# A recurrence's capping and its own-term product move from VectorE to GpSimd, in a one-core AdaLN, attention and FFN kernel

## The reference, cut to what matters

```python
def bi_wkv(r, k, v, w, u, time_emb):          # called with k = v = fside
    ek  = exp(min(k, 30.0))
    ekv = ek * v
    # forward and reverse scans over the 512 positions:
    #   a = a * decay + ekv_t ;  b = b * decay + ek_t
    euk = exp(min(u + k, 30.0))
    num = nf + nb - ekv + euk * v
    den = df + db - ek + euk
    return sigmoid(r) * num / max(den, 1e-8) * gain

x = x + attention(bi_wkv(x, fside, fside, w1, u1, cond), w_qkv, w_o)
x = x + ffn(bi_wkv(x, fside, fside, w2, u2, cond), w_gate, w_up, w_down)
```

## Time and profile before

| | |
|---|---|
| median of 3 runs | 939.11 us (938.11 to 940.47) |
| the profiled execution, its own time | 939.99 us |
| its span, first to last instruction | 938.3 us |
| mean granted TensorE clock | 0.922 of full speed |
| time outside the span | 1.7 us |

### The profile page before, as it was taken

One profiled execution on the slowest core, in us unless ns is written; L12 is line 12 of the kernel. 1 busy time (PEld: TensorE's weight loads), 2 busy tenths in 40 slices (PEclk: granted clock), 3 DMA queues, 4 the chain that ended last, 5 costly groups with the idle time before them and its releaser, 6 DMA issues.

```text
span 938.3 us, 10306 instructions
## 1 busy us (share of the span) xinstructions
PE 752.8 (80%) x3752; PEld 372.9 (40%) x3793; DVE 767.3 (82%) x1057; ACT 468.7 (50%) x694; POOL 73.5 (8%) x149
## 2 busy tenths in 40 slices
PE   2646617698879899897898998877989999995756
PEld 1212203245544344454443444544434446552322
DVE  2999998989997779889978798799877995525466
ACT  5755644448665262476653624766536234441330
POOL 1000000111100002111000021110000211100000
PEclk9777757999999999999999999999999999998778
DMA  8622210445400003654000036540000373300001
GB/s 316 250 67 95 101 56 12 101 102 159 100 12 23 1 12 90 191 146 113 12 23 1 12 89 191 147 113 12 23 1 12 80 190 90 90 1 0 1 0 45
DMA packets 30306, 72.25 MB, mean 77 GB/s; under 512 B 5808, under 2 KB 5808, under 8 KB 28464
## 3 DMA queue, kind: packets, MB, share of 16 engines
q1 hardware_dynamic: 19792, 46.94, 17.0%
q0 software_dynamic: 6144, 16.79, 7.6%
q10 hardware_dynamic: 4320, 7.87, 2.5%
HBM read 33.82 MB, written 4.19 MB: 41 GB/s over the span
## 4 chain that ended last, share of the span: by engine, by line
PE 42%; DVE 31%; issue 9%; ACT 7%; DMA 6%; SPq 4%; POOL 1%; DVEq 0%; ACTq 0%
PE bank L1308 12%; DMA stacks<-rows 5%; PE bank L1320 5%; PE bank L1247 4%; PE bank L1161 4%; PE bank L1236 4%; PE bank L1218 3%; SPq L300 3%; DVE negmax L963 3%; PE bank L1187 2%; ACT region L504 2%; PE bank L1220 2%; DVE fn L847 2%; PE bank L1153 1%; DVE num L861 1%
## 5 line engine op out<-in xcount | busy, mean ns | idle before, releaser
L963 DVE TENSOR_REDUCE negmax<-bank 128x4 f32<-128x512 f32 (+2 forms) x96 | 98.7, 1036 | 40.9 <-PE bank L1194 22.6
L504 ACT ACTIVATE region<-bank 128x384 f32<-128x384 f32 (+1 forms) x192 | 95.5, 523 | 66.1 <-PE bank L1221 63.5
L1218 PE MATMUL bank<-stacks 128*128 128x512 f32 (+3 forms) x256 | 104.8, 416 | 29.2 <-ACT region L504 22.1
L300 POOL DMA_DIRECT2D stacks<-rows x128 | 69.5, 551 | 735.3 <-DVE region L746 351.5
L1161 PE MATMUL bank<-h,wqkv 128*128 128x512 f32 x256 | 115.7, 603 | 7.6 <-DVE region L1114 4.2
L1187 PE MATMUL bank<-stacks 128*128 128x128 f32 (+3 forms) x256 | 81.0, 411 | 10.2 <-DMA stacks<-rows 5.8
L1308 PE MATMUL bank<-region,gate_q 128*128 128x512 bf16 x244 | 62.9, 397 | 23.4 <-DVE region L746 23.0
L1161 PEld LDWEIGHTS bank<-h,wqkv 128*128 128x128 f32 x256 | 48.7, 194 | 66.1 <-issue 55.7
L1218 PEld LDWEIGHTS bank<-stacks 128*128 128x128 f32 x256 | 51.0, 199 | 58.9 <-ACT region L504 39.2
L1114 DVE TENSOR_TENSOR region<-bank,region 128x1024 f32<-128x1024 f32 x32 | 39.1, 1222 | 42.9 <-PE bank L1308 42.9
L1220 PE MATMUL bank<-maxrow,pick 128*128 128x384 bf16 (+3 forms) x236 | 74.0, 314 | 0.0
(11 more groups left out here) (158 smaller groups left out, 1380.4 us busy)
## 6 DMA issues: line engine op xcount, KB each, us to landing
stacks<-rows SPq DMA_DIRECT2D x128, 128.0 KB, 4.0
stacks<-rows POOLq DMA_DIRECT2D x128, 128.0 KB, 4.6
kt<-in_fside ACTq DMA_DIRECT2D x30, 256.0 KB, 3.2
h<-in_x SPq DMA_DIRECT2D x4, 1024.0 KB, 5.7
region<-in_w_gate SPq DMA_DIRECT2D x4, 1024.0 KB, 11.7
xt<-in_x SPq DMA_DIRECT2D x4, 1024.0 KB, 7.5
region<-in_w_up SPq DMA_DIRECT2D x4, 1024.0 KB, 5.7
region<-in_w_down SPq DMA_DIRECT2D x4, 1024.0 KB, 4.7
```

What stands on the lines that cost most here:

```text
L300: eng.dma_start(stacks[HD * r:HD * r + HD, at:at + 2, i, :].bitcast(F32), rows[mine, q:k + 1:k - q, :]).then_inc(stacked[s][i], 16)
L504: nc.scalar.activation(probs[:, i, P_AT[tiles[0]]:P_AT[tiles[0]] + columns], bank[4 + n % 2][:, 0:columns], ACT.Exp, scale=SCALE).then_inc ...
L963: nc.vector.tensor_reduce(o, scored, AX_X, ALU.max, negate=True).then_inc(max_taken, 1)
L1218: nc.tensor.matmul(o, ks[s][:, i, P * t:P * t + P], qs[s][:, i, P * t:T], start=True, stop=False, skip_group_check=True)
```

## The change

On POOL two functions are new. `cap` moves there from DVE as it was. `own_product` caps `eu` in place and writes the product with k over the tile of k; it needs `ekv_ready`, since DVE's `ekv = ek * k` must have read k first. On DVE `add_own` keeps two plain additions. ACT's `load_k` may overwrite k only after `num` has been summed, and moves behind `reciprocals`, at every place where the two stand together. `own_exp` waits also for the product of the unit before. DVE's `ekv = ek * k` no longer waits for `num_ready`.

```diff
+            def cap(b, u):
+                if not live(b, u):
+                    return
+                U = unit(b, u)[2]
+                pool.wait_ge(k_in[u % 2], k_loaded(b, u))
+                if U:
+                    pool.wait_ge(fwd_ready, 2 * U)
+                nc.gpsimd.tensor_scalar(ek[:, :], kt[:, u % 2, :], EXP_CAP, None, ALU.min).then_inc(capped, 1)
+
+            def own_product(b, u):
+                if not live(b, u):
+                    return
+                U = unit(b, u)[2]
+                pool.wait_ge(eu_ready, U + 1)
+                nc.gpsimd.tensor_scalar(eu[:, :], eu[:, :], CAPPED_EXP, None, ALU.min).then_inc(eu_capped, 1)
+                pool.wait_ge(ekv_ready, U + 1)
+                pool.wait_ge(eu_capped, U + 1)
+                nc.gpsimd.tensor_tensor(kt[:, u % 2, :], eu[:, :], kt[:, u % 2, :], ALU.mult).then_inc(euv_ready, 1)
+
+            cap(-1, CJ)
+            for u in range(CJ, 2 * CJ + 1):
+                own_product(-1, u)
+                cap(-1, u + 1)
+            own_product(-1, 9)
+            cap(-1, 10)
             pool.wait_ge(setup, SETUP_STEPS)
             pool.wait_ge(quartered, 2 * WC + 2)
             stack(pool, 0, 0, 2, HG)
+            own_product(-1, 10)
+            cap(-1, 11)
             for b in range(B):
                 pool.wait_ge(down_ready, 1 + b)
                 stack(pool, b, 1, 2, HG)
+                own_product(b, 3)
+                cap(b, 4)
                 stack(pool, b, 2, 2, HG)
+                own_product(b, 4)
+                cap(b, 5)
+                own_product(b, 5)
+                cap(b, 6)
                 stack(pool, b, 3, 2, HG)
+                for u in range(6, 11):
+                    own_product(b, u)
+                    cap(b, u + 1)
                 if b + 1 < B:
                     pool.wait_ge(iq_ready, b * FC + 2)
                     stack(pool, b + 1, 0, 2, HG)
...
                 if U:
                     act.wait_ge(summed, U)
+                    act.wait_ge(euv_ready, U)
                 nc.scalar.activation(eu[:, :], kt[:, u % 2, :], ACT.Exp,
...
-                    act.wait_ge(summed, unit(b, u)[2] + 1)
+                    act.wait_ge(num_ready, unit(b, u)[2] + 1)
                     act.dma_start(kt[:, u % 2, :], fside_tile(b, u + 2)).then_inc(k_in[u % 2], 16)
...
+                reciprocals(b, 4)
                 load_k(b, 4)
-                reciprocals(b, 4)
                 own_exp(b, 5)
...
                     if U:
-                        dve.wait_ge(num_ready, U)
+                        dve.wait_ge(fwd_ready, 2 * U)
                     nc.vector.tensor_tensor(ekv[:, :], ek[:, :], kt[:, u % 2, :], ALU.mult).then_inc(ekv_ready, 1)
...
-                dve.wait_ge(eu_ready, U + 1)
-                nc.vector.scalar_tensor_tensor(ekv[:, :], eu[:, :], CAPPED_EXP, kt[:, u % 2, :], ALU.min, ALU.mult).then_inc(euv_ready, 1)
+                dve.wait_ge(eu_capped, U + 1)
                 dve.wait_ge(bwd_ready, 2 * U + 1)
-                nc.vector.scalar_tensor_tensor(den[:, :], eu[:, :], CAPPED_EXP, den[:, :], ALU.min, ALU.add).then_inc(summed, 1)
+                nc.vector.tensor_tensor(den[:, :], eu[:, :], den[:, :], ALU.add).then_inc(summed, 1)
                 dve.wait_ge(euv_ready, U + 1)
                 dve.wait_ge(bwd_ready, 2 * U + 2)
-                nc.vector.tensor_tensor(num[:, :], num[:, :], ekv[:, :], ALU.add).then_inc(num_ready, 1)
+                nc.vector.tensor_tensor(num[:, :], num[:, :], kt[:, u % 2, :], ALU.add).then_inc(num_ready, 1)
```

More of the change, by code:

```diff
@@ L187, in adaln_attention_ffn @@
         eu_ready = sem("eu_ready")
+        eu_capped = sem("eu_capped")
         fwd_ready = sem("fwd_ready")
@@ L525, in turn @@
                 low_parts(b, 1)
+                reciprocals(b, 2)
                 load_k(b, 2)
-                reciprocals(b, 2)
                 own_exp(b, 3)
@@ L538, in turn @@
                 exps(b, 0, 5, 8)
+                reciprocals(b, 3)
                 load_k(b, 3)
-                reciprocals(b, 3)
                 own_exp(b, 4)
@@ L564, in turn @@
                 copy_maxima(b, 2)
+                reciprocals(b, 5)
                 load_k(b, 5)
-                reciprocals(b, 5)
                 own_exp(b, 6)
@@ L575, in turn @@
                 exps(b, 2, 9, 12)
+                reciprocals(b, 6)
                 load_k(b, 6)
-                reciprocals(b, 6)
                 own_exp(b, 7)
@@ L587, in turn @@
                 exps(b, 3, 6, 12)
+                reciprocals(b, 7)
                 load_k(b, 7)
-                reciprocals(b, 7)
                 own_exp(b, 8)
@@ L594, in turn @@
                 cap_exp(b, 9)
+                reciprocals(b, 8)
                 load_k(b, 8)
-                reciprocals(b, 8)
                 own_exp(b, 9)
@@ L676, in _ @@
                 else:
+                    reciprocals(-1, u)
                     load_k(-1, u)
-                    reciprocals(-1, u)
                     own_exp(-1, u + 1)
@@ L689, in _ @@
                 if n % 2 == 0:
+                    reciprocals(-1, n // 2 + 4)
                     load_k(-1, n // 2 + 4)
-                    reciprocals(-1, n // 2 + 4)
                     own_exp(-1, n // 2 + 5)
@@ L821, in decay @@
                 return decay_all[:, batch_of(b, u), CJ * second + j:CJ * second + j + 1]
[L823 to L829, removed]
-                    dve.wait_ge(fwd_ready, 2 * U)
-                nc.vector.tensor_scalar(ek[:, :], kt[:, u % 2, :], EXP_CAP, None, ALU.min).then_inc(capped, 1)
             def forward(b, u, f):
@@ L898, in _ @@
             ch = Chain(dve, wq_steps, 0, 0)
-            cap(-1, CJ)
             top_magnitude(ch, 0, True)
@@ L913, in _ @@
                         finish(-1, u - 1)
-                    cap(-1, u + 1)
                 else:
@@ L925, in _ @@
                     forward(-1, 8, c)
-                elif c == 2:
-                    cap(-1, 9)
             backward(-1, 8, 0)
@@ L942, in _ @@
                         finish(-1, 8)
-                    cap(-1, 10 + k // 2)
                 round_weights(ch, first + k, first, rounded(first + c))
@@ L1012, in turn @@
                 late_lows(b)
-                cap(b, 4)
                 maxima(b, 1, 0)
@@ L1026, in turn @@
                 finish(b, 3)
-                cap(b, 5)
                 backward(b, 4, 0)
@@ L1039, in turn @@
                 maxima(b, 2, 3)
-                cap(b, 6)
                 backward(b, 5, 0)
@@ L1053, in turn @@
                 finish(b, 5)
-                cap(b, 7)
                 backward(b, 6, 0)
@@ L1066, in turn @@
                 finish(b, 6)
-                cap(b, 8)
                 backward(b, 7, 0)
@@ L1074, in turn @@
                 finish(b, 7)
-                cap(b, 9)
                 normalise(b, 3)
@@ L1099, in turn @@
                         forward(b, 9, 1)
-                        cap(b, 10)
                     else:
@@ L1123, in turn @@
                         forward(b, 10, f - 3)
-                    elif f == 5:
-                        cap(b, 11)
                 raise_top(b, FJ // 2 - 1)
```

## The result

The changed kernel takes **962.53 us** (median of 4 runs, 959.86 to 964.5) against 939.79 us for the kernel before in the same session (4 runs): a ratio of 1.0242, 95% interval 1.0212 to 1.0272. It is slower by 2.4%. 961 had been forecast.

What follows compares the result with a forecast made beforehand. VectorE (82% busy) and PE (80%) share the chain; VectorE counts in the weight stage and attention. Weight stage 4.1 plus three turns of 6.0 gave 22.1 on 939.99, 962.1; the median 0.9 lower, 961 us; range 926 to 980.

Steps and rivals of the forecast that it cites:

- rivals A: Whole kernel: no exclusion beyond the two-port forms, GpSimd's work hidden everywhere; 12.5 us faster, 927 us; chance 0.24.
- C's every-microsecond price: Whole kernel, upper end of the main case: VectorE pays every GpSimd microsecond, 2.52 us a unit; +47, 986 us.
- B's picture: Whole kernel: exclusion, but VectorE keeps the turn and GpSimd waits; 4.7 us faster, 934 us; chance 0.13.
- The rule of exclusion: GpSimd instructions reading SBUF and VectorE instructions with two SBUF inputs run one after the other; full VectorE pays GpSimd's length.
- 0.63 us for a tensor_scalar: Each one-tile GpSimd instruction of 128x512, estimated from mask rows at 0.87 ns a column; 2.33 us a unit with the product.
- my upper end: GpSimd's time per unit at most 2.52 us, taking the product as twice a one-tile instruction.
- Weight stage +4.1: Weight stage: six units, 14.0 us of GpSimd, charged 9.3 less the gain of 5.2 us.
- Turn, 413 to 459, +1.9: Attention stretch of each turn: 8.7 us of GpSimd, half charged as 4.35, less the gain of 2.45 us.
- 459 to 485, +0.5: Units 7 and 8 in each turn: PE's stretch, VectorE has slack until the last normalisation; 0.5 us lost.
- Attention's end +1.6: Each turn: unit 9's capping and product delay the second scan and unit 10's cap, so ACT waits 1.6 us.
- Rounding +2.0: Each turn's rounding: 2.33 us of GpSimd fall on back-to-back VectorE work; fourth piece has slack 0.1; 2.0 us lost.
- Waits and order at no cost: Later load of k, the added wait and copies behind caps cost nothing; closest, the copies after unit 6's cap, about 1 us late.

Runs made afterwards that it cites:

- the idle products and tensor_scalars: Kernel before plus GpSimd instructions nobody reads in the weight stage: 946.79 us with both kinds, 943.55 with products only, 947.04 with tensor_scalars only.
- the middle units alone: Changed kernel with the weight stage's units and each turn's two end units back on VectorE: 935.21 us, ratio 0.9969; repeated, 936.93 us.
- nothing moved: Changed kernel with all caps and own products back on VectorE, leaving only the new order on ScalarE: 944.39 us, ratio 1.0071 to the kernel before.

## Why the prediction was right, and which terms were not

The time (961 against 962.5), the sign and the mechanism held; rivals A and B fell, C's every-microsecond price too, though B's picture, VectorE going on and GpSimd kept waiting, is what most tensor_scalars show. But that the sum came so near is luck: several terms were wrong and cancelled, and 5.1 us of clock stood in none. By its steps:

- **The rule of exclusion, both tiles in SBUF.** Held: the idle products and tensor_scalars stretch VectorE with no dependence between them, and the maxima from PSUM did not change. The Trainium skill (SBUF — State Buffer, Who interferes with whom) has whichever of the two comes first hold the shared ports for its whole instruction; the trace agrees nearly for the product (the scan behind it is stretched by 1.0 of its 1.28 us) and not for the tensor_scalar, 1.48 us long, of which VectorE pays 0.3 to 0.5.
- **0.63 us for a tensor_scalar.** Mis-sized: the mask's slope does not carry over. Unhindered it takes 1.48 to 1.49 us, and 1.97 to 2.04 on average. The product, 1.07 in the forecast, takes 1.27; the 1.07 has a slip in it, for half a column's time more than 0.63 is 0.85, and only a whole one's gives 1.07. The unit is 4.2 us unhindered, not 2.33, above my upper end. The two errors, too short and too fully charged, met in a similar charge: 2 x 0.48 + 0.77 = 1.7 us a unit by the idle instructions.
- **Weight stage +4.1.** It was +7.0 at its end. The first unit's cap at the program's start and the last unit's instructions were left out of the six units that I counted; seven products and eight caps run there.
- **Turn, 413 to 459, +1.9, and 459 to 485, +0.5.** It was nothing: from the turn's first row to the last split of the maxima 82.7 us before and 82.6 after in turn 1, and 250.4 and 249.5 over the three turns. VectorE is still nearly full there (lengths and columns as in the earlier trace rows):

```profile
433.00:473.00 40.00, 30.73 (x236) 17.23 (x234) 38.52 (x47) 24.34 (x46) 16.26 (x15) 0.96 0.29 74
```

So the charge and the gain came out level there, where 4.35 against 2.45 had been forecast. The kernels with the middle units alone show the same for all turns: moving these is no loss.
- **Attention's end +1.6.** It was 2.44. The chain has the links that were written, but the second scan was not pushed back by 1.7: it came 0.4 us later, kept its 1.19, and the product waited for it (2.24 us). The cap stood behind the product and started about where it had been forecast, by luck; it takes 1.49 us, not 0.63, and that is the missing 0.84, nearly.
- **Rounding +2.0.** It was 1.7, by 1.06 for the product and 0.29 for each tensor_scalar.
- **Missing: the granted clock.** F took 5.1 us over three turns, which no term held. TensorE's mean clock over the 35 us that hold the gate and up products was 1.00 in 16, 0.95 in 14 and 0.90 in none of the 30 turns of the ten kernels whose idle time before them was 2.3 to 3.4 us. In the four kernels with 3.5 to 4.7 us it was 1.00 in none, 0.95 in 5 and 0.90 in 7 of 12. In the changed kernel it was 0.90 in all three. So a longer wait at attention's end seems to be paid twice. The two go together, but no run varied the wait alone: the four kernels are also the ones with the end units' products on GpSimd. Within the first group the same idle time goes with either value; what decides there stays open.
- **Waits and order at no cost.** Not so for the order on ScalarE: with nothing moved the kernel is 0.7% slower. The copies behind the cap of unit 6 start 53.2 us into turn 1 and did 53.0 into it before, so they were not late.

In numbers: 4.1 + 3 x (1.9 + 0.5 + 1.6 + 2.0) = 22.1 was forecast. Measured is 7.0 for the stage, 0.5 for A, 7.3 for B, 5.0 for R and 5.1 for F, 24.9, less 2.2 for the last turn and the pieces between the cuts.

## What to carry to other kernels

Moving VectorE work to GpSimd is worth nothing by the count of busy time: here 35.3 us removed came back as 45.1 us of stretch. Ask of each moved instruction what it runs beside and who waits for it: under attention, where part of VectorE's work reads PSUM and no one waits for the moved one, it did no harm; one that a single exponential waited for cost its extra length, and the kernels with the longest such waits lost TensorE's clock behind it as well. Move the units in the slack and keep the ones that close a stage. And run the reordering without the move: 0.7% lay here in what I had costed at nothing.

## What the runs showed of the hardware

- A 128x512 float32 tensor_scalar on GpSimd took 1.48 us alone, 2.24 beside a VectorE scan and up to 4.08 beside VectorE's rounding, whose own instructions gained only 0.29 us. The slowing is very uneven, and mostly GpSimd's.
- A product on GpSimd that reads two tiles (1.27 us) holds up VectorE's one-tile `cap` as well, 1.40 us instead of 0.43, and a 2048-column operation on two tiles, 3.35 instead of 2.29; but a VectorE scan already under way goes on at 1.22 us, and the product ends 0.8 to 1.1 us after it.
- TensorE's mean granted clock over the 35 us from 10 us after B's end took three values only, 1.00, 0.95 and 0.90, with F at 27.7 to 27.9, 29.2 to 29.6 and 29.9 to 30.9 us. Nothing between them occurred in the 42 full turns of the 14 kernels.
